# The merged stage of a transformer layer: a new order inside each step, and a bias that ScalarE writes into PSUM

## What is computed

```python
x = x + _layernorm(attn(_layernorm(x)))          # attn ends in  out @ w_out + b_out
y = _layernorm(x)
shared = (silu(y @ sfc1.T) * (y @ sfc2.T)) @ sfc3.T   # 512 hidden columns
logits = y @ gate_w.T                            # 16 experts
top_w, top_idx = top_k(logits, 2); top_w = softmax(top_w)
moe = sum over the two chosen experts of top_w * (silu(y @ w1[e].T) @ w2[e].T)
x = x + _layernorm(moe + shared)
```

## Time and profile before

| | |
|---|---|
| runs, us | 873.39, 873.05, 870.5 (median 873.05) |
| the profiled execution, us | 871.27 |
| its span, first to last instruction, us | 869.4 |
| mean granted TensorE clock over the span | 0.969 of full speed |
| busy share of the span: PE, PEld, DVE, ACT, POOL | 88%, 55%, 75%, 60%, 43% |

### The profile page before, as it was taken

The page is one execution under the profiler, slowest core; times in us unless marked ns, Lnnn a source line. Parts: engine busy times, 40 slices in busy tenths (PEclk is TensorE's granted clock), DMA queues, the critical chain, the costliest instruction groups (busy, mean ns, idle before and its releaser), DMA issues. The chain is left out here.

```text
span 869.4 us, 14912 instructions
## 1 busy us (share of the span) xinstructions
PE 765.8 (88%) x4690; PEld 475.3 (55%) x4690; DVE 649.5 (75%) x1256; ACT 521.7 (60%) x1047; POOL 370.9 (43%) x442
## 2 busy tenths in 40 slices
PE   4579999999999999999888769999998799998883
PEld 3444444444444434344333347778777688887773
DVE  4488989899898897998798547877864355554785
ACT  2217777778777787777677644343342477775463
POOL 4350271551713616326100012565674177775541
PEclk9959999999999999999999989999999799999998
DMA  8874549657586577574865012444466456665995
GB/s 163 234 154 100 122 79 240 138 166 186 98 198 156 144 185 150 142 176 78 192 146 196 2 53 86 135 128 150 138 206 184 129 181 186 180 213 176 289 157 97
DMA packets 112340, 133.28 MB, mean 153 GB/s; under 512 B 16644, under 2 KB 80646, under 8 KB 112264
## 3 DMA queue, kind: packets, MB, share of 16 engines
q1 hardware_dynamic: 98536, 108.39, 49.8%
q0 software_dynamic: 13248, 23.15, 10.2%
q10 hardware_dynamic: 480, 0.79, 0.6%
HBM read 68.18 MB, written 59.87 MB: 147 GB/s over the span
## 5 line engine op out<-in xcount | busy, mean ns | idle before, releaser
L485 DVE TENSOR_REDUCE negmax<-ring 128x2 f32<-128x1024 f32 x256 | 304.6, 1209 | 52.7 <-PE ring L648 52.1
L435 ACT ACTIVATE probs<-scores 128x512 f32<-128x512 f32 x498 | 272.0, 599 | 79.8 <-PE scores L666 79.0
L666 PE MATMUL scores<-q_st,k_st 64*128 64x512 f32 x498 | 202.3, 464 | 20.4 <-ACT probs L435 15.9
L648 PE MATMUL ring<-k_st,q_st 48*128 48x512 f32 x512 | 180.6, 464 | 11.9 <-DMA k_st<-rows_in 7.3
L666 PEld LDWEIGHTS scores<-q_st,k_st 64*128 64x128 f32 x498 | 81.3, 186 | 162.0 <-ACT probs L435 110.6
L680 PE MATMUL av<-probs,v_aug 128*32 128x512 f32 x1024 | 137.5, 609 | 6.3 <-ACT probs L435 6.3
L648 PEld LDWEIGHTS ring<-k_st,q_st 48*128 48x128 f32 x512 | 69.6, 191 | 19.8 <-DMA q_st<-rows_in 8.8
L336 POOL CAST part_r<-negmax 128x16 fp32r<-128x16 f32 x32 | 8.3, 260 | 163.5 <-DVE negmax L485 163.5
L1539 POOL DMA_INDIRECT rows_out<-m_y,projected x48 | 47.3, 986 | 43.5 <-ACT m_y L1599 35.8
L1692 DVE TENSOR_REDUCE m_g<-ring 128x256 f32<-128x512 f32 x40 | 27.7, 692 | 46.8 <-PE ring L1772 45.6
L167 POOL TENSOR_TENSOR scratch<-qk_raw,cos 128x512 f32<-128x512 f32 x29 | 37.1, 1281 | 59.1 <-ACT qk_raw L388 57.1
(11 more groups left out here) (253 smaller groups left out, 1622.2 us busy)
## 6 DMA issues: line engine op xcount, KB each, us to landing
q_st<-rows_in SPq DMA_DIRECT2D x96, 128.0 KB, 4.3
k_st<-rows_in SPq DMA_DIRECT2D x90, 128.0 KB, 4.3
experts<-split SPq DMA_DIRECT2D x8, 1024.0 KB, 5.9
projected<-records SPq DMA_DIRECT2D x48, 129.0 KB
split<-O SPq DMA_DIRECT2D x24, 256.0 KB, 3.3
experts<-rows_out SPq DMA_DIRECT2D x10, 512.0 KB, 8.0
m_rows<-records SPq DMA_DIRECT2D x32, 129.0 KB, 2.5
X<-in_x SPq DMA_DIRECT2D x8, 512.0 KB, 5.2
```

The lines of the kernel that those rows point to most:

```text
L435: nc.scalar.activation(probs[r // 2 % 2][r % 2][:, a, :], score_of(R)[:, a, :], ACT.Exp, scale=HD ** -0.5).then_inc(exp_done, 1)
L485: nc.vector.tensor_reduce(negmax[Gn % 2][:, t, 2 * p:2 * p + 2], ring[t % 2][:, :, :], AX.X, ALU.max, negate=True).then_inc(max_done, 1)
L648: last = nc.tensor.matmul(half[:, a, :], q[rows, t * P:(t + 1) * P], k[rows, :], start=True, stop=True)
L666: nc.tensor.matmul(score_of(R)[:, a, :], k[rows, kt * P:(kt + 1) * P], q[rows, :], start=True, stop=True).then_inc(sc_ps, 1)
```

## The change

Four things are changed, all in the merged stage.

1. The bias leaves the projection for s > 0. A tile `bias_rows` holds the bias in full precision (a view of the tile `wide`, filled once by a sum on GpSimd), and ScalarE copies it into both halves of `bank_y` before the projection accumulates into them (`bias_into`, two copies of 128x512). The wait for `z1_s` moves from TensorE to ScalarE; TensorE waits for `biased_s`.
2. TensorE's order in a step: `first(a)` goes before `gate`, and `logits` goes between the two halves of `first(b)`.
3. GpSimd's order: three of the four k = 0 scatters go ahead of `first_scale`, the other five scatters between it and `powers`.
4. VectorE and ScalarE are reordered to match: `multiply(a)` ahead of the second statistics, `multiply(b)` ahead of `scale_of_mean`, `hidden(b)` ahead of `second_norm`, `logits_out` after `hidden(a)`, and `counts` and `ends` to the start of step 9.

```diff
         for k in both:
             if s > 0:
-                pe.wait_ge(z1_s, s * QT - 2 + 2 * k)
+                pe.wait_ge(biased_s, 2 * s - 1 + k)
...
-                for j, bias in enumerate(part(small, BIAS, D)):
+                for j, bias in enumerate(part(small, BIAS, D) if s == 0 else ()):
...
+    def bias_into(act, s):
+        if not live(s):
+            return
+        for k in range(2):
+            act.wait_ge(z1_s, s * QT - 2 + 2 * k)
+            nc.scalar.copy(bank_y[k].rearrange("p (t d) -> p t d", d=D), bias_rows.unsqueeze(1).broadcast_to([P, 2, D])).then_inc(biased_s, 1)
...
             for s in range(1, LAST + 1):
+                scatter(s - 2, 0, 0)
+                scatter(s - 2, 1, 0, (0,))
                 if live(s):
                     first_scale(pool, s)
-                scatter(s - 2, 0, 0)
-                scatter(s - 2, 1, 0)
+                scatter(s - 2, 1, 0, (1,))
+                scatter(s - 2, 0, 1)
+                scatter(s - 2, 1, 1)
                 if live(s) or live(s - 1):
                     powers(pool, s)
-                scatter(s - 2, 0, 1)
-                scatter(s - 2, 1, 1)
...
             second_norm(act, 0)
+            act.wait_ge(bias_s, 1)
+            bias_into(act, 1)
...
-                if live(s - 1):
-                    logits_out(s - 1)
                 rows_high(act, s + 1)
...
                 if early(a):
                     hidden(a)
+                if live(s - 1):
+                    logits_out(s - 1)
                 if early(b):
                     silus(b)
+                bias_into(act, s + 1)
+                if early(b):
+                    hidden(b)
                 if live(s):
                     second_norm(act, s)
-                if early(b):
-                    hidden(b)
...
                 slot_rows(s - 2)
+                if s == LAST:
+                    counts()
+                    ends()
...
                 rows_low(dve, s + 1)
+                if early(a):
+                    multiply(a)
                 if live(s):
                     second_statistics(dve, s)
                 if early(a):
-                    multiply(a)
+                    hidden_low(a)
                 if live(s - 1):
                     best_two(s - 1)
-                if s == LAST:
-                    counts()
-                    ends()
-                if early(a):
-                    hidden_low(a)
-                if live(s - 1):
                     choices(s - 1)
...
+                if early(b):
+                    multiply(b)
                 if live(s):
                     scale_of_mean(dve, s)
-                if early(b):
-                    multiply(b)
...
                 products(nc, bank_a[:, :], [(weight(S1 + c * S + n * P, P), turned[c]) for c in range(DC)]).then_inc(a_s, 1)
+                between()
...
+                first(a)
                 gate(s - 1)
-                if s > 0:
-                    first(a)
-                logits(s - 1)
-                if s > 0:
-                    first(b)
-                    second(a)
+                first(b, lambda: logits(s - 1))
+                second(a)
```

More of the change, by code:

```diff
@@ L806, in feed_forward @@
         asem(x) for x in "gate lt lg gap ratio taken route both wts rank slot".split())
+    bias_s, biased_s = asem("bias"), asem("biased")
     first_rows, copied, scattered = ([asem(f"{x}{i}") for i in range(2)] for x in ("first_rows", "copied", "scattered"))
@@ L1063, in feed_forward @@
         wide = sbt("wide", [P, E, NT])
+        bias_rows = wide[:, 0:D // NT, :].rearrange("p e t -> p (e t)")
         passed, passed_sum, owner = sbt("passed", [P, 2, E]), sbt("passed_sum", [P, 2]), sbt("owner", [P, 2])
@@ L1113, in gpsimd, with scatter @@
             pool.wait_ge(consts, 3)
-            def scatter(b, i, k):
+            pool.wait_ge(small_in, 16)
+            nc.gpsimd.tensor_tensor(bias_rows.rearrange("p (a r) -> p a r", r=P), *(x.bitcast(F32) for x in part(small, BIAS, D)), ALU.add).then_inc(bias_s, 1)
+            def scatter(b, i, k, of=(0, 1)):
                 if not live(b):
@@ L1125, in scatter @@
                     pool.wait_ge(copied[i], 32 * (b + 1))
-                for j in range(2):
+                for j in of:
                     t = b * QT + 2 * i + j
@@ L1382, in rank, with first @@
                 last.then_inc(rank_s, 1)
-            def first(m):
+            def first(m, between=lambda: None):
                 if not early(m):
+                    between()
                     return
```

## The result

The changed kernel took 863.55 us (median of 6 runs, 860.88 to 867.08) against 873.49 us for the kernel before beside it: ratio 0.9896, 95% interval 0.9866 to 0.9925. The forecast was 861.4 in a range of 856.5 to 866.5. The profiled execution, the fastest of the six, has a span of 859.1 us where before had 869.4.

The account below looks back on a forecast made before the run. TensorE was taken to bound the merged stage, busy 16.43 of 17.77 us a step. Terms 0 - 8.3 - 1.4 + 1.1 - 2.2 = -10.8 us gave 860.5 or 862.2 by base; forecast 861.4, range 856.5 to 866.5.

Parts of the forecast that it names:

- The period: Merged stage, steps 2 to 6: 16.1 us a step against 17.77, no longer set by TensorE; -8.3 us.
- loop A: VectorE's slot_rows, three GpSimd scatters, first_scale, then VectorE from residual_rows to the next slot_rows: 16.04 us.
- Loop B: Through GpSimd: eight scatters between slot_rows and powers, needed before the next slot_rows; 15.72 us, 16.10 with one scatter delayed.
- TensorE's floor: What TensorE alone needs per merged-stage step once the bias and two waits are taken off: 15.5 us.
- Step 1: Start of merged stage: later projection +2.5 us, less low-clock time -1.6, stalls gone -0.8; together about 0.
- Step 7: Merged stage, a step without rows_low: 14.96 us against 16.40, -1.4 us.
- Step 8: Merged stage: TensorE sits 2.1 to 2.7 us ahead of turn(7), against 1.1 us idle before; +1.1 us.
- Rival 2: The clock falls in step 8 after its new idle time, costing 2.5 us: about 864; chance 0.16 together with rival 1.
- The tail: Merged stage's end: earlier counts remove TensorE's 1.83 us wait and bring SP's zeroing forward; together -2.2 us.
- rival 3: GpSimd's scatters are blocked by every VectorE sum, loop B 18.3 us: +2.2 us, about 874.5; chance 0.06.
- 4: Rival: eight GpSimd scatters in a row cost 1.64 us each, loop B 18.7: +6.3 us, about 879; chance 0.07.
- rival 1: Only the bias counts, TensorE's waits return elsewhere: period 16.79 us, -7.0, about 865; chance 0.16 together with rival 2.

Follow-up runs that it names:

- e1: The changed kernel with GpSimd's old order (first_scale, four scatters, powers, four scatters): 858.55 us, ratio 0.9825.
- e2: The changed kernel with the bias back on TensorE and without ScalarE's copies: 865.26 us, ratio 0.9907.
- e8: The kernel before with only the bias moved to ScalarE, all orders as before: 869.69 us, ratio 0.9974.
- e7: The changed kernel with GpSimd's old order, no GpSimd wait for scatters at the stage's end, and the bias on TensorE: 865.22 us, ratio 0.9929.
- e9: The changed kernel once more, unaltered, in a later set of runs: 865.33 us, ratio 0.992.
- e10: The changed kernel with GpSimd's old order, repeated on one chip with the changed kernel: 859.80 us, ratio 0.9857.
- e6: The changed kernel with GpSimd's old order and without GpSimd's wait for its scatters at the stage's end: 860.99 us, ratio 0.9877.
- e11: The changed kernel with GpSimd's old order and no GpSimd wait at the stage's end, repeated on one chip: 860.31 us, ratio 0.9876.
- e4: The changed kernel with counts and ends back late in step 9, behind multiply(16): 861.57 us, ratio 0.9879.
- e3: The changed kernel without GpSimd's wait for its own scatters at the stage's end; SP still waits for them: 860.55 us, ratio 0.987.
- e5: The changed kernel with TensorE's old order, all other engines as changed: 880.31 us, ratio 1.0097.

## Why the prediction was right, and where it was not

**The period, right.** 15.9 us for 16.1. Two errors of loop A cancelled in part: the semaphore into GpSimd took 0.28 us, not 0.1, and the gap of 0.30 behind the third scatter falls away when `first_scale` follows. Loop B had room: `powers` starts 0.52 us after the last scatter has ended. That the loop, and not TensorE, sets the step was argued; e1 showed it by opening the loop. TensorE's floor was put 0.5 too high, because idle times were taken off and not the time from start to start. Rows of step 3 before, and two of step 4 after:

```profile
556.37 0.40 PE L738 MATMUL misc<-shared,a_h_hi 128*128 128x256 f32 x2
...
563.24 0.40 PE L738 MATMUL scores<-a_t_hi,shared 128*128 128x512 f32 x1
...
565.70 0.39 PE L738 MATMUL scores<-a_t_hi,shared 128*128 128x512 f32 x1
566.16 0.39 PE L738 MATMUL av<-shared,a_h_lo 128*128 128x256 f32 x1
```

```profile
576.46 0.39 PE L738 MATMUL scores<-a_t_hi,shared 128*128 128x512 f32 x1
576.69 0.28 PE L738 MATMUL av<-shared,a_h_lo 128*128 128x256 f32 x1
```

Products of 512 columns follow each other at 0.23 us, those of 256 at 0.12. By that pitch the stop ahead of 564.42 cost 0.95 us and not 0.79, the one ahead of 557.24 cost 0.63 and not 0.48, and `second(a)` began 0.23 late, which no bracket lists and which is gone after the change. Together that is 0.54, and 15.5 becomes 15.0.

**The bias, right in place, and its price depends on the loop.** The copies are hidden in steps 2 to 7 (0.57 us each where 0.61 was taken). The same 0.98 us of matrix work was worth 0.13 a step where GpSimd's loop sets the period (e2), 0.68 in the old order (e8), 0.95 where TensorE does (e7).

**Step 1, forecast 0, was the granted clock's.** The same kernel took 19.29 us at a mean clock of 0.85 and, in e9, 21.95 at 0.72, after the same 5.28 us of idle time. In e9 the clock fell to 0.50 again from 532 to 534 us, after 2.02 us of idle time ahead of `first(a)`; in the first profile it stayed at 1.00 after 2.33. e10 and e1 (19.44 and 21.93 us) and e6 and e11 (19.46 and 21.95) differ in the same way. The three profiles with the bias on TensorE (before, e2, e7) have the higher clock here, 0.85 to 0.86; whether the longer wait makes the low one likelier was not tried.

**Step 7, mis-sized by 0.5.** The term took 1.14 us off loop A, but TensorE is busy for 15.04 of the 15.52 us and waits 0.48: without `rows_low` TensorE bounds this step, by these numbers; no run tests it.

**Step 8, mis-sized in this profile by 1.1, and near in e9.** Rival 2 happened, at 1.5 us instead of 2.5: the clock fell after the new idle time. In e9 it did not, after an idle time that was the same within 0.01 us. What decides between the two was not settled.

**The tail, the term that failed.** The step that failed is "that chain ends near 22 us after `rank(7)` and no longer ends last; what is left is TensorE's own end". SP's chain did end sooner, but what was left was GpSimd: its wait for the scatters, whose landing took longer beside the zeroing (e4), and then 5.30 us of drain (e3). It is the last in all four profiles of kernels that keep this wait together with GpSimd's new order and the early counts (the changed kernel, e9, e2, e5). Before, that drain had ended 0.1 us before SP's began, so nothing that shortened SP's chain alone could gain more than 0.2 us there. The median was in the range all the same, since the period gained 1.2 more than forecast and, in the profiles, the third stage 2.1 to 2.2, for which the sum has no term. That part is luck. In e9 the gain beside the kernel before was 5.7 us, less than the 8.5 at which the forecast begins.

**The third stage** was between 188.1 and 194.2 us in the profiles of these runs, and goes by and large with the granted clock. Its first 20 us in the kernel before, the changed kernel and e3:

```profile
676.45:696.45 20.00, 17.75 (x106) 15.84 (x107) 8.66 (x16) 9.39 (x22) 4.59 (x5) 0.74 0.48 131
```

```profile
668.35:688.35 20.00, 17.41 (x117) 15.46 (x118) 10.08 (x18) 10.76 (x27) 5.91 (x6) 0.85 0.49 134
```

```profile
670.33:690.33 20.00, 16.80 (x127) 14.74 (x128) 10.39 (x19) 11.40 (x28) 6.61 (x7) 1.00 0.48 145
```

TensorE gets through 106, 117 and 127 products in them; the stage took 192.95, 190.75 and 188.07 us. These 20 us don't settle it alone: e4 had 1.00 there and took 190.95, and e1 had 0.86 and took 193.7, with 0.91 in its last 93.6 us where e3 had 0.96 in its last 88. Whether the change has a part in that clock was not tried.

**The rivals.** 3 and 4 did not come, and of rival 1 only that a wait on `a_lt` appeared; its time, by the two bases of the sum, is 864.3 to 866.1, not 865 to 866. Of the scatters shown, the one at 572.96 starts 0.10 us ahead of the end of `rows_low` and takes its 0.96; the one at 651.88, in step 9, starts inside `hidden_low`, 651.75 to 652.44, and takes 1.39. That second one is as the rule cited in the prediction has it (the Trainium skill, SBUF — State Buffer, Who interferes with whom). The other half of the rule as the prediction words it, that the sum is blocked where it came second, the trace does not bear out: `rows_low` at 571.84 starts inside the scatter of 571.70 and takes 1.22 us, as before. A scatter lost 0.12 to 0.13 us less than the sum had left: 0.38 of 0.50 at 561.21, 0.43 of 0.56 at 651.88, nothing of 0.10 at 572.96. In steps 2 to 6 of the new order scatters start inside `rows_low` only in its last 0.1 us and never inside `hidden_low`, so rival 3 had no ground there. The version to keep is neither kernel but that of e1 and e10: 858.55 and 859.80 us, ratios 0.9825 and 0.9857.

## What to carry to other kernels

When a queue is reordered, follow the loop that the order closes through every engine and price it from starts; then build the change without that part too, since one part of a good change can take back a third of what the others bring (5 of 14 us here). A saving is worth its full price only on the engine that sets the period: measure it there. At the end of a stage list every engine's last wait and drain; shortening the one that ends last gains no more than its lead over the next.

## What the runs showed of the hardware

- GpSimd's drain at the end of the merged stage took 5.30 us in every run in which GpSimd had waited for its scatters first, and 9.88 to 16.33 us where it had not (e3, e6, e7, e11); VectorE's took 0.72 to 0.73, ScalarE's 1.02, SP's 0.13 to 0.14.
- Behind a scatter the next scatter starts after 0.30 us, but a compute instruction after 0.01 (569.10 to 569.11); from a compute instruction to a scatter it takes 0.19.
- A scatter that starts while VectorE runs a sum over two SBUF tiles took 0.43 us longer than its 0.96 (651.88); a sum that starts while a scatter runs took no longer (571.84).
- The last four scatters of the stage landed 6.0 to 8.0 us after their issue (medians of five profiles) where the zeroing of 16 tiles had begun before them, and 4.4 us after it where it began when two of them had started (e4).
- Idle times of 2.26 and 2.25 us in the same place of one kernel were followed by a granted clock of 0.50 once and of 1.00 once; idle times of 2.06 us, of another, by a mean clock of 0.89 (e1) and 1.00 (e10) in the step.
